# 4-bit FFN weights unpacked during the attention, through table rows gathered by GpSimd and f32 weights in device memory

## What is computed

```python
# layer 0: cross attention, 32 query heads, 8 key/value heads of 128
q, k, v = latents @ Wq, kv @ Wk, kv @ Wv          # kv = [context, latents]
q, k = rms_norm(q, q_norm_w), rms_norm(k, k_norm_w)
x = x + softmax(q k^T / sqrt(128)) v @ Wo
# layer 0: FFN with 4-bit weights (512 -> 1376 -> 512)
w = (qweight[:, None, :] >> shifts & 15).reshape(-1, n)      # 8 numbers in one int32
z = (qzeros >> shifts & 15) + 1
W = (w - z[g_idx]) * scales[g_idx]                # groups: 4 for gate and up, 10 for down
x = x + (silu(layernorm(x) @ Wg) * (layernorm(x) @ Wu)) @ Wd
# layer 1: attention of the context over the tokens, then a linear map with 8 low-rank experts
```

## Time and profile before

| | |
|---|---|
| time, median of 3 runs | 1183.19 us (1180.73 to 1184.94) |
| the profiled execution's own time | 1182.78 us |
| its span, from first to last instruction | 1181.0 us |
| TensorE busy | 1121.7 us, 95% |
| VectorE busy | 751.9 us, 64% |
| ScalarE busy | 541.7 us, 46% |
| GpSimd busy | 416.3 us, 35% |
| DMA engines, mean share | 17.3% |

### The profile page before, as it was taken

One profiled execution on the slowest core, in us unless ns is written; L12 is line 12 of the kernel. 1 busy time (PEld: TensorE's weight loads), 2 busy tenths in 40 slices (PEclk: granted clock), 3 DMA queues, 4 the chain that ended last, 5 costly groups with the idle time before them and its releaser, 6 DMA issues. The chain is left out here.

```text
span 1181.0 us, 19222 instructions
## 1 busy us (share of the span) xinstructions
PE 1121.7 (95%) x6643; PEld 959.8 (81%) x6643; DVE 751.9 (64%) x1572; ACT 541.7 (46%) x1437; POOL 416.3 (35%) x421
## 2 busy tenths in 40 slices
PE   4899999999999999999999998789999999988998
PEld 3798998998998998998998887657768777676877
DVE  6555555555555555555555677789874566789863
ACT  4445445445445445445445454333332445465631
POOL 4442332332332332332332442144431333485521
PEclk9999999999999999999999999999999999999999
DMA  6211011011011011011010020023212225244300
GB/s 213 77 36 33 23 37 32 24 37 32 24 36 32 23 37 32 24 37 32 24 30 11 1 70 1 9 63 81 81 47 54 63 49 121 72 90 99 80 11 36
DMA packets 48716, 56.49 MB, mean 48 GB/s; under 512 B 10822, under 2 KB 29270, under 8 KB 48620
## 3 DMA queue, kind: packets, MB, share of 16 engines
q1 hardware_dynamic: 48620, 55.26, 17.3%
HBM read 40.56 MB, written 2.10 MB: 36 GB/s over the span
## 5 line engine op out<-in xcount | busy, mean ns | idle before, releaser
L379 PE MATMUL bank<-wqkv,kvT 128*128 128x256 f32 x1536 | 201.3, 288 | 8.7 <-DVE vv L567 8.7
L424 PE MATMUL bank<-wo,aoT 128*128 128x512 f32 x768 | 193.6, 401 | 5.6 <-DVE acc L563 5.6
L379 PEld LDWEIGHTS bank<-wqkv,kvT 128*128 128x128 f32 x1536 | 189.5, 193 | 10.4 <-DVE vv L567 10.4
L367 PE MATMUL bank<-wqkv,kvT 128*128 128x512 f32 x768 | 188.8, 395 | 1.7 <-DVE qn L577 1.7
L424 PEld LDWEIGHTS bank<-wo,aoT 128*128 128x128 f32 x768 | 140.6, 190 | 33.8 <-DVE aoT L558 6.3
L367 PEld LDWEIGHTS bank<-wqkv,kvT 128*128 128x128 f32 x768 | 141.7, 191 | 28.9 <-issue 1.8
L663 POOL TENSOR_TENSOR rms<-msq,half_neg 128x4 f32<-128x4 f32 x64 | 64.5, 1008 | 220.5 <-DVE msq L574 220.3
L666 POOL TENSOR_TENSOR rms<-msq,half_neg 128x2 f32<-128x2 f32 x64 | 44.6, 697 | 133.5 <-DVE msq L583 133.5
L550 ACT ACTIVATE prob<-bank,nmax 128x128 f32<-128x128 f32 x256 | 90.3, 372 | 2.1 <-DVE nmax L587 2.1
L875 PE MATMUL bank<-x2T,wgu 128*128 128x512 f32 (+1 forms) x336 | 90.3, 413 | 0.0
L528 ACT ACTIVATE qsq<-bank 128x512 f32<-128x512 f32 x64 | 38.2, 597 | 112.8 <-PE bank L367 112.8
(11 more groups left out here) (181 smaller groups left out, 2203.8 us busy)
## 6 DMA issues: line engine op xcount, KB each, us to landing
wqkv_raw<-in_L_xattn_Wq_dram SPq DMA_DIRECT2D x32, 256.0 KB, 2.5
wo_raw<-in_L_xattn_Wo_dram SPq DMA_DIRECT2D x32, 256.0 KB, 2.7
qS<-qhl SPq DMA_DIRECT2D x32, 256.0 KB, 3.7
kS<-chl SPq DMA_DIRECT2D x32, 128.0 KB, 3.1
packed<-_L_ffn_gate_qweight_dram SPq DMA_DIRECT2D x40, 64.0 KB, 2.3
packed<-in_L_ffn_up_qweight_dram SPq DMA_DIRECT2D x40, 64.0 KB, 2.3
packed<-_L_ffn_down_qweight_dram SPq DMA_DIRECT2D x10, 256.0 KB
acc<-in_x_dram SPq DMA_DIRECT2D x8, 256.0 KB, 5.7
```

The source lines that it names most:

```text
L367: mm = pe.matmul(b_q[:, :], kvT[:, l, kt, p, 1:3, :], wqkv[:, par, r, kt, 0:QW], start=(kt == 0 and n == 0), stop=(kt == KT - 1 and n == 2))
L379: mm = pe.matmul(b_kv[:, b * 256:(b + 1) * 256], kvT[:, l, kt, p, 2 * b:2 * b + 2, :], wqkv[:, par, r, kt, QW:QKV], start=(kt == 0 and n = ...
L424: mm = pe.matmul(b_o[:, :], aoT[:, l, h, :, :], wo[:, par, r, h, :], start=(h == 0 and n == 0), stop=(h == G - 1 and n == 2))
```

## The change

The blocks of 4-bit weights are unpacked during the attention and no longer in the FFN's first half.

- The spreading matmuls, the 0/1 matrices, the tables in SBUF and all that makes them are taken out.
- Zeros (plus 1) and scales are written to small tables in device memory, one row for each group: zeros beside scales. This takes small VectorE operations at the ends of steps 1 to 3 and DMAs of SyncE (sp_tables, sp_quantized).
- There are 35 blocks (chunk): 24 of up to 128 x 512 for gate and up, 11 of 128 x 512 for down. For each, an indirect DMA issued by GpSimd after its L666 gathers 128 rows of up to 1024 floats (gather_row); SyncE loads the packed block, each row eight times; VectorE makes three operations (dequant), at two places of a step from step 5 on: before L572 ("q"), and before L577, where it waits for GpSimd ("rq"); SyncE stores the f32 block. Block c is done in step 5 + (3c + 2) // 2, the last one in step 57.
- SyncE issues the attention's weight pieces one for each step (weight_load), after that step's stores and loads.
- In the FFN, weight_tile loads the f32 weights of one tile (three DMAs of 256 KB, three tiles deep); ScalarE makes the high part (three of 128 x 512), VectorE the low part (GpSimd for tile 0).
- The turn from the attention to the FFN is in a new order: transposes of the normed x, and inner_product(0, 0) and (0, 1) stand between the last products of the attention (steps 64 to 66), xn2 has four buffers in place of two, and the layer-norm statistics of the pairs have other steps.

The core of the diff:

```diff
+                    n = 4 * (g + 1) + t // 2 + 2          # weight_load(j), g, t = divmod(j, 8)
+                    if n < 4 * KVH:
+                        qkv_piece(n // 4, n % 4, n - 1)
...
+            sp_tables(sp)
+            for j in range(STEPS0 - 6):
+                sp_quantized(sp, j)
+                weight_load(j)
...
+            if st.j == UNITS:
+                pe.wait_ge(s_qT, UNITS)
+                pe.wait_ge(s_kT, UNITS)
+                x2_transposes(pe, 0)
+                x2_transposes(pe, 1)
...
+            if st.j > UNITS and st.j < UNITS + 3:
+                inner_product(pe, 0, st.j - UNITS - 1)
...
+        def gather_row(pool, j):
+            for c in range(CHUNKS):
+                if j != (FIRST - 1 if c < 2 else done_step(c - 2)):
+                    continue
+                k, _, b, w, rows_, col = chunk(c)
...
+                if c >= 2:
+                    pool.wait_ge(s_deq, 3 * (c - 2) + 3)
+                pool.indirect_dma_start(rows[0:rows_, c % 2, 0:2 * w], None, table[k, b][:, :],
+                                        bass.IndirectOffsetOnAxis(idx[0:rows_, col:col + 1], 0)).then_inc(s_row[c % 2], 16)
...
+        def dequant(dve, c, step):
+            _, _, _, w, rows_, _ = chunk(c)
+            q = qch[0:rows_, c % 2, 0:w]
+            if step == 0:
...
+                dve.tensor_scalar(q, q, shift[0:rows_, 0:1], 15, ALU.logical_shift_right, ALU.bitwise_and).then_inc(s_deq, 1)
+            elif step == 1:
+                dve.wait_ge(s_row[c % 2], 16 * (c // 2 + 1))
+                dve.wait_ge(s_deq, 3 * c + 1)
+                dve.tensor_tensor(q.bitcast(F32), q, rows[0:rows_, c % 2, 0:w], ALU.subtract).then_inc(s_deq, 1)
             else:
+                dve.wait_ge(s_deq, 3 * c + 2)
+                dve.tensor_tensor(q.bitcast(F32), q.bitcast(F32), rows[0:rows_, c % 2, w:2 * w], ALU.mult).then_inc(s_deq, 1)
...
+        def weight_tile(sp, f):
+            w = width(f)
+            if f >= 3:
+                sp.wait_ge(s_wlo, 3 * (f - 2))
+            for k in range(2):
+                sp.dma_start(wload[:, f % 3, k, :].rearrange("p (t n) -> p t n", t=KT)[:, :, 0:w],
+                             w_gu[f, :, k, :, 0:w]).then_inc(s_w_in[f % 3], 16)
+            sp.dma_start(wload[0:w, f % 3, 2, :], w_d[f * P:f * P + w, :]).then_inc(s_w_in[f % 3], 16)
...
-                if kt == KT // 2 - 1 and n >= 1:
-                    spread_next(pe, n, 2 * m)
             mm.then_inc(done, 1)
-            if n >= 1:
-                spread_next(pe, n, 2 * m + 1)
```

More of the change, by code:

```diff
@@ L715, in width, with chunk @@
             return min(P, F - f * P)
[L717 to L721, removed]
+        def chunk(c):
+            if c < 2 * KT * BLOCKS:
+                i, b = divmod(c, BLOCKS)
+                return i // KT, i % KT, b, min(D, F - b * D), P, i
+            f = c - 2 * KT * BLOCKS
+            return 2, f, 0, D, width(f), 2 * KT + f
@@ new lines, in sp_quantized @@
+        def sp_quantized(sp, j):
+            if j == 2:
+                sp.wait_ge(s_zi, 9)
+                for k, (m, n, g) in enumerate(WEIGHTS):
+                    sp.dma_start(z_line[k].rearrange("g c -> (g c)").rearrange("(p c) -> p c", c=64),
+                                 qch[0:g * n // 64, 0, k * 64:(k + 1) * 64].bitcast(F32)).then_inc(s_line, 16)
+            if j == 3:
+                sp.wait_ge(s_line, 48)
+                for k, (m, n, g) in enumerate(WEIGHTS):
+                    for b in range(-(-n // D)):
+                        w = min(D, n - b * D)
+                        sp.dma_start(table[k, b][:, 0:w], z_line[k][:, b * D:b * D + w]).then_inc(s_tab, 16)
+                quantized_load(sp, 0)
+                quantized_load(sp, 1)
+            for c in range(CHUNKS):
+                if j == done_step(c) + 1 and c + 2 < CHUNKS:
+                    quantized_load(sp, c + 2)
+            for c in range(CHUNKS):
+                if j == done_step(c):
+                    weight_store(sp, c)
@@ L723, in sp_ffn @@
         def sp_ffn(sp):
+            for c in (CHUNKS - 2, CHUNKS - 1):
+                sp.wait_ge(s_w_out[c % 2], stored(c))
+            sp.wait_ge(s_wo, 4 * KVH)
             sp.wait_ge(s_q, EVEN_DONE)
             sp.wait_ge(s_kv, EVEN_DONE)
[L726 to L731, removed]
@@ L732, in sp_ffn @@
-            sp.wait_ge(s_zero_v, 18)
-            for f in range(FT):
[L734 to L747, removed]
+            for f in range(FT):
+                weight_tile(sp, f)
@@ L900, in pe_ffn, with whole_down @@
         def pe_ffn(pe):
-            def whole_down(n, now):
-                down(pe, n, (0, 1))
-                spread_next(pe, now, 4)
-                down(pe, n, (2, 3)).then_inc(s_d, 1)
-                spread_next(pe, now, 5)
+            def whole_down(n):
+                down(pe, n, range(HP)).then_inc(s_d, 1)
             for n in range(FT + ALONE):
@@ L1113, in dve_ffn @@
                 if n == FT - 1:
-                    for p in (HP, HP + 1):
-                        ln_apply(dve, X2, p, xn2[:, p % 2, :])
+                    for p in range(HP, PAIRS):
+                        ln_apply(dve, X2, p, xn2[:, p % HP, :])
                 if n == FT:
```

480 lines of the change are left out of this document (210 added, 270 removed).

## The result

The changed kernel takes 1144.76 us (median of 4 runs, 1143.53 to 1144.92) against 1182.95 us for the kernel before on the same chip (4 runs, 1180.73 to 1184.94): ratio 0.9674, 95% interval [0.9658, 0.969]. So it is 38.2 us faster. The profiled execution took 1143.53 us with a span of 1141.7. The forecast was 1141, 3.8 us too low, inside its range of 1136 to 1148.

What follows compares the result with a forecast made beforehand. TensorE was taken to bound the attention and the FFN's first half, idling between them. Gains 11.6 + 16.5 + 13.3 + 1.0 less 0.6 make 41.8 us, from 1182.8 to 1141 us; range 1136 to 1148.

Steps and rivals of the forecast that it cites:

- Steps 58 to 63: Attention's last steps: with VectorE's table work gone from their ends, 78.1 us become 66.5, a gain of 11.6 us.
- The turn: Attention to FFN, step 64 to inner_product(1, 0): 38.5 us become 22 in the new order, a gain of 16.5 us.
- Some 4 us: In the turn: the gain lost again if VectorE's order holds up each of the three output products as before.
- FFN, first half: Ten tiles without spreading matmuls, 8.36 us each: 96.9 us become 83.6, gain 13.3 us, if TensorE stays the bound.
- the f32 tiles bind: Rival, FFN's first half: loads stay at 75 GB/s where 92 are needed, no gain there, 1154 us; chance 4%.
- Turn to the second half: Within the FFN: four buffers remove the third transpose's 1.69 us wait; gain 1 us, 0 to 2.5 with a slow-clock stretch.
- The start: Eight small operations on zeros at the ends of steps 1 and 2 cost 0.6 us (0 to 2).
- four operations of 0.15 us cost 0.6 us: End of step 1, where there is no slack before step 2's key projection: the small operations cost 0.6 us.
- slack of 2.04 us: Free time at a step's end, 1.17 us before L558 plus 0.87 us before the key projection; to cover steps 2 and 3.
- The attention: Unpacking and gathers in 53 steps fit the gaps of VectorE and GpSimd: cost 0; gather taken as 2 us.
- the collision that I counted at 0.6 us a step: At "rq", VectorE's operation meets GpSimd's power: qn ends about 0.6 us later, covered by idle time; uncovered, 32 us.
- All behind: Everything after the turn to the FFN's second half is unchanged: 0 us.

Runs made afterwards that it cites:

- turn_plain: Changed kernel with inner_product(0, 0) and (0, 1) moved from between the attention's last output products to behind them; 1146.12 us.
- spread_back: Changed kernel with twelve bf16 matmuls of 256 columns, results unused, put back into each of tiles 1 to 9 of the FFN's first half; 1155.78 us.
- zlate: Changed kernel with the small VectorE operations on zeros and indices moved from the ends of steps 1 to 3 to a gap in steps 3 to 5, blocks two steps later; 1138.77 us.
- gather8: Changed kernel with seven more gathers of 128 rows of 32 bytes, into a scratch tile, ahead of each of the 35; 1272.09 us.
- deq_twice: Changed kernel with each of the 105 unpacking operations followed by a second of the same size; 1144.37 us.

## Why the prediction came out

Of the 3.8 us by which the forecast was too low, 2.5 lie between the two profiles' spans (39.3 gained for 41.8); the rest is the distance of the medians from the profiled executions. The 2.5 are partly luck: 0.9 lost at the start and 2.8 behind the FFN, against 1.4 won at the turn to the second half.

*Steps 58 to 63: right.* 11.6 us forecast and found; each step is 11.08 us at most, so the norm's remaining work fits in the slack. No run puts the table work back; that it was the cause is read from the two traces.

*The turn: right, with one part underrated.* 16.6 us against 16.5. Both waits that I had at 0.5 us are there: 0.59 us before inner_product(0, 0), and 0.41 before inner_product(1, 1), which lies behind the end of this window and so in the next. "Some 4 us" was my price for output products that VectorE holds up; in turn_plain it is 5.2, and 1.6 us of that is a product at 1.2 GHz behind the first wait, which I had not counted.

*FFN, first half: right.* 83.95 us against 83.6, the difference being the 0.41 us for hval, and spread_back shows the cause. The rival "the f32 tiles bind" did not come: TensorE is busy for 83.54 of the 83.95 us, while the DMAs moved 70 GB/s and not 92, since three tiles had been asked for before.

*Turn to the second half: 2.4 in place of 1.0.* The wait went from 1.69 to 1.32 us and a second one of 0.40 is gone: 0.8 us. The rest is mostly the slow stretch that I had as the end of the range: the product of 96 rows behind the wait took 4.22 us before, at a granted clock of 0.68 in the mean (0.50 from 885 to 888), and takes 3.00 us now at 1.00 (the row at 844.74), 1.2 us. Why the clock fell there before and does not now is not shown beyond the shorter wait.

*The start: mis-sized.* The step "four operations of 0.15 us cost 0.6 us" failed. The operations took 0.37 and 0.53 us each in the mean because they meet GpSimd's weight piece, which I had not looked for there. Step 2 became 1.4 us longer, and step 3, which I had covered by the slack of 2.04 us, 0.7. The cost was 2.1 us, 1.5 of it visible in the table since step 2 began 0.6 us early. zlate shows it by moving them.

*The attention: right.* No step from 4 on pays. I took 2 us for the gather and it is 1.03; the free time before a cost is 6.5 to 7.6 us by gather8, where I had 7.4. L671, all 64 of them, went from 64.5 us to the 79.9 of this row of the groups:

```profile
L671 POOL TENSOR_TENSOR rms<-msq,half_neg 128x4 f32<-128x4 f32 x64 | 79.9, 1248 | 234.4 <-DVE msq L581 234.2
```

That is the collision that I counted at 0.6 us a step; it is 0.4 us where both meet, and deq_twice shows that twice the work is absorbed too. The rule of the Trainium skill (SBUF — State Buffer, Who interferes with whom) on two SBUF inputs agrees with that row. The other rule cited from the Trainium skill, on small reads for each gather index (GPSIMD Engine Reference, Performance pitfalls for Q7 kernels), would have made an estimated 10.9 us of a gather; the trace has 1.03 us for 128 rows, so it does not price this instruction, and the measurement decides.

*All behind: 0 forecast, 2.8 us lost.* The code there is the same, and so are the counts: 1374 matmuls and 388 instructions of VectorE. The granted clock is 0.98 where it was 0.99. Two places show it. In the changed kernel TensorE idles until 1094.66, and then its granted clock is 0.50 from 1095 to 1098:

```profile
1094.66 0.88 PE L1438 MATMUL bank<-ident,pr 128*128 128x128 f32 x4 [1.54 <-POOL pr L1975]
```

Two windows, the second of them behind that row and the first around an earlier fall of the clock; the granted clock is third from the end:

```profile
995.83:1008.94 13.11, 10.51 (x56) 8.99 (x55) 9.61 (x22) 7.48 (x18) 9.05 (x10) 0.74 0.51 116
1094.66:1101.37 6.71, 6.71 (x35) 5.90 (x35) 2.88 (x6) 2.10 (x4) 0.00 (x0) 0.75 0.10 39
```

The kernel before idles 1.53 us at the same program place:

```profile
1135.41 0.66 PE L1462 MATMUL bank<-ident,pr 128*128 128x128 f32 x4 [1.53 <-POOL pr L1999]
```

And keeps its clock there: 1.00 in the last of these windows. The first is all that lies behind the FFN, the second is the place of the earlier fall:

```profile
903.62:1181.00 277.38, 259.47 (x1374) 206.53 (x1372) 189.30 (x388) 127.41 (x288) 115.42 (x124) 0.99 0.30 72
1037.96:1049.66 11.70, 9.09 (x55) 7.83 (x54) 9.63 (x22) 7.53 (x18) 8.98 (x10) 0.85 0.57 130
1135.41:1140.62 5.21, 5.21 (x35) 4.55 (x35) 2.77 (x6) 2.10 (x4) 0.00 (x0) 1.00 0.13 50
```

That is 6.71 - 5.21 = 1.5 us. At the other place both kernels' clocks fall, the changed kernel's from 999 to 1006 and the other's from 1042 to 1045: 13.11 - 11.70 = 1.4 us. Each of the three parts of the stretch around and between these places is as long as before, within 0.1 us. So the whole loss is the two falls. Over ten profiles whose code is the same there, the stretch took 277.4 us (before), 277.9, 278.1, 278.2, 278.3, 278.9, 280.1, 280.2 (after), 280.3 and 280.7, and both profiles of the changed kernel have both falls. What decides at such an idle stretch whether the clock falls was not found, and stays open; that the change as such causes the 2.8 us is not shown, since zlate, which has all of it, is at 277.9.

## What to carry to other kernels

Before new work is put beside a full engine, look at what the *other* engines do in the very microseconds it lands in: the same four operations took 0.42 us and cost nothing in one gap, and took 1.5 and 2.1 us at another place, which cost the kernel 2.1 us in all. Work that an engine's queue must do at a fixed place (a gather, an unpacking) is free up to a sum that can be read from the gaps, and beyond it nearly every step with such work pays, here more than the excess, since the clock falls too; so read the threshold and stay far below. And where the last products of one stage wait for a sum, products of the next stage put between them gain twice: the wait itself, and the clock behind it (3.3 and 1.6 us here).

## What was not expected of the hardware

- Small one-input VectorE operations on SBUF (96x24) wait for a GpSimd tensor operation: 1.49 and 2.10 us for four of them in place of 0.42.
- A gather's address writing does not hold VectorE's two-input operations up: 0.69 us amid gathers, 2.25 us beside a GpSimd tensor operation. On GpSimd a gather of 128 rows took 1.03 us, and further ones 0.95 us each with 0.31 us between; data of 4 KB a row lay in SBUF 3.9 to 5.3 us after the issue.
- An idle stretch of 1.53 to 1.54 us at the same place of the program was followed by a granted clock of 1.00 in one profile and of 0.50 in another.
